# A recommender tower on one core: its dense layers in chunks of four units, sums turned to rows through memory

## What is computed

```python
e = jnp.stack([tbl_f[ids[:, f]] for f in range(16)], axis=1)      # 512 x 16 x 256
for i in range(3):
    z = jnp.einsum('bfe,bge->bfge', x, xk).reshape(B_, F_ * F_, E_)
    z = jnp.swapaxes(z, 1, 2)
    z = jnp.einsum('bcl,oc->bol', z, Ws[i]) + bs[i][None, :, None]
    z = jax.nn.relu(z)
    z = jnp.sum(z, axis=-1)
    outs.append(z)
    xk = jnp.broadcast_to(z[:, :, None], (B_, F_, E_))
h = jnp.concatenate([z, dense_ctx], axis=1)                       # 48 sums and 16 dense features
h = jnp.maximum(h @ W_top1 + b_top1, 0.0)                         # 64 -> 512
h = jnp.maximum(h @ W_top2 + b_top2, 0.0)                         # 512 -> 256
y = h @ W_top3                                                    # 256 -> 1
```

## Time and profile before

| | |
|---|---|
| median of 3 runs | 171.51 us (171.51 to 172.08) |
| the profiled execution | 171.46 us, span 169.6 us |
| PE busy | 137.1 us (81%) |
| DVE busy | 144.9 us (85%) |
| ACT busy | 126.3 us (74%) |
| POOL busy | 121.0 us (71%) |
| mean granted PE clock | 0.99 |

### The profile page before, as it was taken

One profiled execution on the slowest core, in us unless ns is written; L12 is line 12 of the kernel. 1 busy time (PEld: TensorE's weight loads), 2 busy tenths in 40 slices (PEclk: granted clock), 3 DMA queues, 4 the chain that ended last, 5 costly groups with the idle time before them and its releaser, 6 DMA issues.

```text
span 169.6 us, 6453 instructions
## 1 busy us (share of the span) xinstructions
PE 137.1 (81%) x2728; PEld 92.4 (54%) x2728; DVE 144.9 (85%) x136; ACT 126.3 (74%) x441; POOL 121.0 (71%) x84
## 2 busy tenths in 40 slices
PE   0045998988887878787879797999898999993995
PEld 0024665746464646464646464757474876763963
DVE  3169986999999999999999999999999998198330
ACT  3020465586979797979797979798999998977461
POOL 1777989898888888888888888989797995000000
PEclk9999999999999999999999999999999999999599
DMA  2343653131313030303030303031313100000000
GB/s 56 94 123 97 190 151 97 30 98 37 93 33 95 25 101 12 112 9 117 2 114 10 103 20 103 24 99 35 96 32 97 31 4 4 6 0 2 4 0 0
DMA packets 5273, 9.98 MB, mean 59 GB/s; under 512 B 2179, under 2 KB 2947, under 8 KB 5252
## 3 DMA queue, kind: packets, MB, share of 16 engines
q0 software_dynamic: 3072, 8.39, 17.2%
q1 hardware_dynamic: 2036, 1.29, 2.8%
q10 hardware_dynamic: 144, 0.00, 0.0%
HBM read 9.68 MB, written 0.00 MB: 57 GB/s over the span
## 4 chain that ended last, share of the span: by engine, by line
PE 46%; DVE 19%; ACT 18%; issue 8%; POOL 4%; DMA 3%; DVEq 1%; ACTq 0%
PE Y L627 25%; DVE PR L311 13%; ACT prod L387 8%; ACT XT L357 7%; PE T L592 5%; POOL X L329 4%; PE T L688 4%; PE ZB L648 4%; DVE prod L503 3%; PE Y L633 2%; ACT Y L378 2%; PE YD L670 2%; DMA X<-in_table,idx 2%; PE YD L688 2%; PE YD L604 1%
## 5 line engine op out<-in xcount | busy, mean ns | idle before, releaser
L311 DVE TENSOR_TENSOR PR<-T,XT 128x1024 f32<-128x1024 f32 (+2 forms) x72 | 101.1, 1450 | 7.0 <-ACT XT L357 6.9
L627 PE MATMUL Y<-PR,w_sb 128*32 128x272 f32 x1024 | 66.0, 399 | 13.0 <-DVE PR L311 12.6
L329 POOL DMA_INDIRECT X<-in_table,idx x64 | 61.2, 956 | 20.7 <-issue 16.1
L387 ACT ACTIVATE prod<-prod,bias_sb 128x256 f32<-128x256 f32 x122 | 60.1, 498 | 4.2 <-DVE prod L503 4.2
L311 POOL TENSOR_TENSOR PR<-XT 128x2048 f32<-128x2048 f32 (+2 forms) x16 | 59.7, 3734 | 0.3
L627 PEld LDWEIGHTS Y<-PR,w_sb 128*32 128x32 f32 x1024 | 31.1, 110 | 35.7 <-issue 12.1
L503 DVE TENSOR_TENSOR prod<-U,ZB 128x2048 f32<-128x2048 f32 (+1 forms) x18 | 35.6, 1982 | 3.4 <-PE ZB L648 3.3
L378 ACT ACTIVATE Y<-Y,bias 128x136 f32<-128x136 f32 x64 | 21.5, 336 | 14.2 <-PE Y L633 14.2
L592 PE MATMUL T<-ident_sb,X 128*128 128x128 f32 x128 | 21.7, 314 | 12.3 <-DMA X<-in_table,idx 12.3
L357 ACT ACTIVATE XT<-T 128x1024 f32<-128x1024 f32 (+1 forms) x17 | 16.6, 974 | 18.1 <-PE T L592 13.2
L592 PEld LDWEIGHTS T<-ident_sb,X 128*128 128x128 f32 x128 | 17.5, 211 | 14.0 <-issue 9.9
(11 more groups left out here) (48 smaller groups left out, 69.3 us busy)
## 6 DMA issues: line engine op xcount, KB each, us to landing
X<-in_table,idx POOLq DMA_INDIRECT x64, 2.8
w_sb<-in_w SPq DMA_DIRECT2D x1, 512.0 KB
w_sb<-in_w SPq DMA_DIRECT2D x1, 224.0 KB
sel_sb<-in_sel SPq DMA_DIRECT2D x1, 128.0 KB
ident_sb<-in_ident SPq DMA_DIRECT2D x1, 64.0 KB, 2.1
w1l_sb<-in_w1l SPq DMA_DIRECT2D x1, 64.0 KB
w2l_sb<-in_w2l SPq DMA_DIRECT2D x1, 64.0 KB
w_sb<-in_w SPq DMA_DIRECT2D x1, 64.0 KB
```

The source lines that it names most:

```text
L311: return eng.tensor_tensor(pr, x0.broadcast_to(shape), x1.broadcast_to(shape), ALU.mult)
L329: pool.indirect_dma_start(out=X[:, n % NV, g, :], out_offset=None, in_=table, in_offset=bass.IndirectOffsetOnAxis(ap=idx[:, NT * n + g:NT ...
L387: last = act.activation(q, q, ACT.Relu, bias=bias_sb[:, l + 1:l + 2], accum_out=to)
L627: pe.matmul(Y[TR * j:TR * j + TR, h, 0:YC], w0_sb[:, c, :], PR[:, v, h, c, CB * j:CB * (j + 1), :].rearrange("q b s -> q (b s)"), start=c ...
```

## The change

- The tower works on four chunks of four units. Chunks 0 and 1 run inside steps 7 to 10 and 11 to 14 (`part` 0 to 3), in a second PE loop; chunks 2 and 3 at the end. The second layer's four matmuls stand between the two contractions of a step, behind a wait for `u_read`.
- For chunks 0 and 1, and in part for 2 and 3, the sums reach `H` by two transfers, SBUF to memory and back as rows (`to_rows` on SP), in place of `select`. The bias of the first layer becomes a row of `w1`.
- The last chunk's second layer is contracted with the samples on the partitions, four matmuls of 256 columns, and DVE makes the third layer in one pass (`weighted`); the output leaves in two writes, the second of 128 rows of one number.
- POOL does no products for units 0 and 1, five rows for units 9 and 14, all eight for the last. After its last products it adds up two stages' products (`FOLDS`), which ACT summed before.
- `prod` has three buffers. PE has idle matmuls (`keep_busy`) at the start. Unit 2 is transposed before unit 1 is contracted. `layer_u` of the last unit is split, the last contractions follow each other, with spreads inside them.

```diff
-POOL_ROWS = {0: 0, NU - 2: 6, NU - 1: 6}
...
+POOL_FIRST = 2
+POOL_ROWS = {9: 5, 14: 5, NU - 1: 8}
...
+ACT_SHARE = {(NU - 2, 0): 2, (NU - 1, 1): 2, (NU, 1): 2, (NU - 3, 1): 0, (NU - 2, 1): 0}
+FOLDS = [(NU - 3, 1), (NU - 2, 1)]
...
+LOOP = range(3, FIRST)
+TOWER_LOOP = range(FIRST, NU - 1)
...
+            def to_rows(k, l, landed):
+
+                sp.dma_start(rows[k, l].rearrange("p (n b) -> p n b", b=SB), sums_of(k)[l])\
+                    .then_inc(sums_out[k], 16)
+                sp.wait_ge(sums_out[k], 16 * (l + 1))
+                sp.dma_start(H[TR * l:TR * l + F, PW * k:PW * (k + 1)].rearrange("q (g i) -> q g i", g=P // F),
+                             rows[k, l].rearrange("(g q) i -> q g i", q=F)).then_inc(landed, 16)
+
+            for k in range(NK):
+                sp.wait_ge(z0_ready, 2 * PC * (k + 1))
+                to_rows(k, 0, h_in if k < LAST else h_last_in)
+                if k < LAST:
+                    wait_sums(sp, (PC * (k + 1) - 1, 0))
+                    to_rows(k, 1, h_in)
+                if k < FLOW:
+                    wait_sums(sp, (PC * (k + 1), 1))
+                    to_rows(k, 2, h_in)
...
+            pool.wait_ge(bias_in, 16)
+            step = 0
+            for s, l in FOLDS:
+                b0 = act_share((s, l))
+                q = prod[:, s % NPR, SB * l + b0:SB * (l + 1), :, :].rearrange("q b f g -> q b (f g)")
+                if (s, l) == FOLDS[0]:
+                    pool.wait_ge(prod_ready, outer_done((s, l)))
+                    pool.tensor_scalar(q, q, bias_sb[:, l + 1:l + 2], 0.0, ALU.add, ALU.max)\
+                        .then_inc(pool_step, 1)
+                    step += 1
+                    pool.wait_ge(pool_step, step)
+                else:
+                    pool.wait_ge(relu_ready, FOLDS.index((s, l)))
+                pool.tensor_tensor(q[:, :, 0:P], q[:, :, 0:P], q[:, :, P:2 * P], ALU.add)\
+                    .then_inc(pool_step, 1)
+                step += 1
+                pool.wait_ge(pool_step, step)
+                pool.tensor_tensor(q[:, :, 0:P // 2], q[:, :, 0:P // 2], q[:, :, P // 2:P], ALU.add)\
+                    .then_inc(folded, 1)
...
+            sum_prod((NU - 4, 1), [0])
+            square(NU - 1)
+            read_behind(NU - 2)
+            read_u(NU - 2)
+            read_u(NU - 1, (0,))
+            sum_y(NU - 2, 0)
+            sum_prod((NU - 4, 1), [1])
+            sum_prod((NU - 3, 0), [0])
+            sum_y(NU - 2, 1)
+            sum_prod((NU - 3, 0), [1, 2, 3])
+            sum_prod((NU - 4, 1), [2])
             sum_y(NU - 1, 0)
-            sum_prod(NU - 2, 0)
+            sum_prod((NU - 2, 0))
+            sum_prod((NU - 4, 1), [3])
             sum_y(NU - 1, 1)
-            evacuate((1, HIDDEN1, 2))
-            evacuate((1, HIDDEN1, 3))
-            sum_prod(NU - 2, 1, [0, 1])
-            sum_prod(NU - 1, 0)
-            sum_prod(NU - 2, 1, [2, 3])
-            sum_prod(NU - 1, 1)
-            sum_prod(NU, 1)
-            evacuate((2, SELECT, 0))
-            evacuate((1, HIDDEN2, 0))
-            evacuate((1, HIDDEN2, 1))
-            evacuate((2, HIDDEN1, 0))
-            evacuate((2, HIDDEN1, 2))
-            evacuate((1, OUTPUT, 0))
-            evacuate((2, HIDDEN2, 0))
-            evacuate((2, OUTPUT, 0))
+            read_u(NU - 1, (1,))
+            relu_prod((NU - 2, 1))
+            read_selected(LAST - 1, 2)
+            sum_prod((NU - 1, 0))
+            read_hidden1(LAST - 1, 0)
+            read_hidden1(LAST - 1, 1)
+            sum_prod((NU - 1, 1))
+            sum_prod((NU, 1))
+            read_selected(LAST, 1)
+            read_selected(LAST, 2)
+            read_hidden2(LAST - 1, 0)
+            for c in range(2):
+                act.wait_ge(hidden1, 2 * LAST + 1)
+                act.activation(h1_of(LAST, c), hidden1_psum(LAST, 0)[:, c, :], ACT.Relu).then_inc(h1_ready, 1)
+            read_hidden2(LAST - 1, 1)
+            read_output(LAST - 1)
...
+            outer(NU - 2, [0], 0)
+            spread_z(NU - 2, 1)
+            spread_z(NU - 1, 0)
+            outer(NU - 2, [1], 1)
+            sum_prod((NU - 2, 0))
+            spread_z(NU - 1, 1)
+            outer(NU - 1, [0], 0)
+            outer(NU - 1, [0], 1)
+            outer(NU - 1, [1], 1)
+            sum_fold((NU - 3, 1))
             spread_z(NU)
-            outer(s, [1])
+            sum_prod((NU - 1, 1))
             outer(NU, [1])
-            sum_prod(NU, 1)
-            evacuate((2, HIDDEN1, 1))
-            evacuate((2, HIDDEN1, 3))
-            evacuate((2, HIDDEN2, 1))
+            sum_fold((NU - 2, 1))
+            sum_prod((NU, 1))
+            dve.wait_ge(weights_in, 16 * 7)
+            dve.wait_ge(hidden1, 2 * LAST + 2)
+            for c in range(2):
+                dve.tensor_scalar(h1_of(LAST, 2 + c), hidden1_psum(LAST, 1)[:, c, :], 0.0, None, ALU.max)\
+                    .then_inc(h1_dve, 1)
+            dve.wait_ge(hidden2, 2 * LAST + 1)
+            dve.scalar_tensor_tensor(out=weighted[:], in0=last_psum, scalar=0.0, in1=w3row_sb[:], op0=ALU.max,
+                                     op1=ALU.mult, accum_out=y_last[:]).then_inc(last_done, 1)
...
+            def step(n, v, r, k=None, part=None):
+
+                contract(n - 1, 1 - v, 0)
+                if isinstance(n, int) and n == 2:
+                    pe.wait_ge(spread_in, 16)
+                spread_rows(n - 2)
+                if part is not None and part >= 1:
+                    pe.wait_ge(u_read, n)
+                if part == 1:
+                    pe.wait_ge(h1_ready, 2 * k + 1)
+                    first_hidden(k, 1)
+                elif part in (2, 3):
+                    pe.wait_ge(h1_ready, 2 * k + 2)
+                    if part == 3:
+                        pe.wait_ge(h2_ready, 2 * k + 1)
+                    second_hidden(k, part - 2)
+                contract(n - 1, 1 - v, 1)
+                transpose(n + 1, 1 - v, r + v)
+                if part == 0:
+                    pe.wait_ge(weights_in, 16 * 7)
+                    pe.wait_ge(dense_in, 16)
+                    pe.wait_ge(h_in, 16 * 3 * (k + 1))
+                    pe.wait_ge(u_read, n)
+                    first_hidden(k, 0)
+                elif part == 1:
+                    pe.wait_ge(h1_ready, 2 * k + 2)
+                elif part == 2:
+                    pe.wait_ge(h2_ready, 2 * k + 1)
+                elif part == 3:
+                    pe.wait_ge(h2_ready, 2 * k + 2)
+                    outputs(k)
+                layer_u(n, v)
...
+            contract(0, 0, 0)
+            layer_u(0, 0)
+            contract(0, 0, 1)
+            transpose(2, 0, 1)
+            layer_u(1, 1)
+            pe.wait_ge(z0_ready, 2)
+            keep_busy(Y[:, 1, 0:P], 7)
...
+            layer_u(NU - 1, last, (0,))
+            contract(NU - 2, 1 - last, 0)
+            spread_rows(NU - 3)
+            contract(NU - 2, 1 - last, 1)
+            contract(NU - 1, last, 0, [(NU - 2, 0)])
+            contract(NU - 1, last, 1, [(NU - 2, 1), (NU - 1, 0)])
+            layer_u(NU - 1, last, (1,))
+            select(LAST - 1, 2)
+            spread_rows(NU - 1, 1)
+            pe.wait_ge(h_in, 16 * (3 * LAST - 1))
+            pe.wait_ge(h_ready, 1)
+            pe.wait_ge(y_done, LAST - 1)
             pe.wait_ge(u_read, NU)
-            for c in range(HC1):
-                tower((1, HIDDEN1, c))
-            spread_rows(NU - 1)
-            n0 = CHUNKS[2][0]
-            select(2, 0, n0, NU)
-            select(2, 1, n0, NU - 1)
-            select(2, 2, n0, NU - 2)
-            tower((1, HIDDEN2, 0))
+            for half in range(2):
+                first_hidden(LAST - 1, half)
             spread_rows(NU)
-            tower((1, HIDDEN2, 1))
-            select(2, 1, NU - 1, NU)
-            select(2, 2, NU - 2, NU).then_inc(mlp_psum[2], 1)
-            for c in range(HC1):
-                tower((2, HIDDEN1, c))
-            tower((1, OUTPUT, 0))
-            for c in range(HC2):
-                tower((2, HIDDEN2, c))
-            wait_sbuf(pe, (1, OUTPUT, 0))
-            tower((2, OUTPUT, 0))
+            pe.wait_ge(h1_ready, 2 * LAST)
+            second_hidden(LAST - 1, 0)
+            second_hidden(LAST - 1, 1)
+            pe.wait_ge(minus_half_ready, 2)
+            pe.matmul(last_psum, ones[:], b2row_sb[:], start=True, stop=False)
+            select(LAST, 1)
+            select(LAST, 2)
+            pe.wait_ge(h_last_in, 16)
+            pe.wait_ge(h_ready, 3)
+            for half in range(2):
+                first_hidden(LAST, half)
+            for q in range(HC1):
+                if q < 2:
+                    pe.wait_ge(h1_ready, 2 * LAST + 1 + q)
+                else:
+                    pe.wait_ge(h1_dve, q - 1)
+                tile = pe.matmul(last_psum, h1_of(LAST, q), w2_sb[:, q, :], start=False, stop=q == HC1 - 1)
+            tile.then_inc(hidden2, 1)
+            pe.wait_ge(h2_ready, 2 * LAST)
+            outputs(LAST - 1)
```

566 lines of the change are left out of this document (286 added, 280 removed).

## The result

The changed kernel takes **179.69 us** (median of 4 executions, 177.99 to 182.07); the kernel before took 171.80 on the same chip (4 executions, 171.51 to 172.10). The ratio is 1.039 with a 95% interval of 1.032 to 1.045: slower. I had said 169.7, 167.3 to 172.6, and 0.15 for slower. The ratios of this document leave out executions that were disturbed; the medians are over all. By mean granted clock the executions are 177.99 and 178.01 us at 0.967 and 0.968, and 181.37 and 182.07 at 0.948; a fifth, for the ratio alone, took 179.39 at 0.958.

A forecast was written before the change was run, and what follows sets the result against it. The prediction took VectorE (DVE) to bound the middle and a dependency chain the tail. From 171.46 us, terms -0.2, +4.0, +0.2, -2.4, -3.1 and +0.2 gave 170.2; half a microsecond off made 169.7, range 167.3 to 172.6.

The forecast's parts named there:

- The output: Final write: 128 rows of 4 bytes in place of one row take between 1.5 and 1.8 us, +0.2.
- The tower's waits: Steps 9, 10, 13, 14: late XT fills make DVE wait 1.3 and 1.1 us, in each of two rounds.
- such a fall in the tail: Tail: PE's clock falls to its lower level after thin work, slowing chunk 2's second-layer matmuls, +1.2 us.
- POOL's fifth row of unit 9: Unit 9's products: POOL takes five rows in place of four, saving DVE 0.57 us.
- The start: First units: more DVE product work, offset by a vanished idle before unit 2 and earlier transposes, -0.2 us.
- Contractions 14 and 15: Last two contractions, back to back with spreads inside: 10.0 us in place of 12.37, -2.4.
- The last chain: End of contractions to output's issue: 15.0 us in place of 18.1, a clock fall of 1.2 included, -3.1.
- rival A: Tail: the clock does not fall, so the kernel takes 168.5 us; chance 0.18.
- The memory pair: Sums written to memory and read back as rows: 4.2 us a pair, PE waits 0.6, +0.2 in all.
- Rival B: Steps 7 and 11: rows arrive late from memory, holding up PE; 171.2 or 173.2 us; chance 0.15.
- POOL's folds: Tail: folds of 2.0, 1.1 and 0.7 us end 2.5 us before DVE reduces, costing nothing.

The follow-up runs named there:

- e1: The changed kernel with its last 128 outputs turned into a row by one matmul and written in one write: 171.98 us, ratio to before 0.999.
- e4: The changed kernel writing its last 128 outputs 64 bytes apart into a scratch tensor: 211.2 us on a chip where the kernel before took 209.73.
- e8: The changed kernel writing its last 128 outputs as 64-byte rows, side by side, to a scratch tensor: 211.2 us where the kernel before took 209.73.
- e13: The changed kernel unedited, on a chip where the kernel before takes about 210 us: 219.44 us, ratio 1.042.
- e14: The changed kernel writing its last 128 outputs 64 bytes apart into a scratch tensor, same edit as e4, beside e13: 212.18 us, ratio 1.008.
- e3: The changed kernel with five idle matmuls ahead of the waits for U in steps 9, 10, 13 and 14: 176.52 us, ratio to before 1.023.
- e5: The changed kernel without the seven idle matmuls ahead of contract (1,0): 177.0 us, ratio to before 1.025.
- e17: The changed kernel with the output written as one row and chunks 0 and 1's second layer behind the transposes: 169.83 us, ratio to before 0.959.
- e18: The kernel of e17 without the seven idle matmuls ahead of contract (1,0): 165.28 us, ratio to before 0.963.

## Why the prediction was wrong

**The step that failed is *The output*.** I put 128 rows of 4 bytes between the output's 1.5 and the 1.8 of bias_sb and added 0.2; it cost 6.4. The bound came from the wrong side: bias_sb is 128 short rows read from memory and written to 128 partitions, this is a write into memory, whose pieces lie side by side. It took e1 to weigh it (6.3 us in the profile, 7.7 in the median with the clock's part), and e4, e8, e13 and e14 to rule out the number and the size of the pieces. This term alone put the time outside the range: with 0.2 true of the write the executions of 178.5 would have been 172.3, and e1 did take 171.98, both within 167.3 to 172.6. But that is no gain, and the long profiled execution would still have been 175.2; that the change is not faster has the reasons that follow.

**The tower's waits were right, but not the clock behind them.** Waits for the late fills: 4.8 predicted, 5.28 with the clock up. What I left out is that the same wait which delays the fill also leaves PE idle for a microsecond in a place where it has little else: I had forecast such a fall in the tail from the earlier trace rows and not asked for it at the waits that the change itself adds. It cost 3.3 us in the profiled execution (e3 against the changed kernel), 3.2 in the medians and 2.0 against the 178.5. Of the other 0.9 in e3's +5.1, 0.28 is unit 13's wait, and some 0.5 is POOL's fifth row of unit 9: the product is shorter (128x1536, 1.76), but zx still comes 8.49 behind the one before (80.78 to 89.27), 0.04 and not 0.57 sooner. The product itself starts only at 87.33, right behind its fill (86.20 to 87.23), and behind it DVE waits 0.19 for sums: there was hardly slack to win.

**The start.** -0.2 holds with the clock up (-0.1 in e3); the profiled execution lost 1.6 there to a fall behind the wait for a gather, which the seven idle matmuls made worse (e5). The kernel's 4 us between shortest and longest go with the mean clock, 0.967 against 0.948; which falls the other executions had, no trace shows.

**Contractions 14 and 15.** -1.8 for -2.4: they take 10.6 us in place of 10.0, and PE waits for nothing in them (busy 10.61 of 10.61 us). The two halves of unit 15, with spreads between their matmuls, take 2.3 and 2.5 by the profile's chain, not counting the spreads, where I had 2.16 each; the three spreads take the 1.1 that I had as 1.0 with waits.

**The last chain.** Both cases that I weighed happened. With the clock up it took 13.5 us (13.7 predicted, rival A), in e5 as well and with the row in e1 13.6; in e3, whose tail is the same code, the granted clock was 0.60 from 158 to 162 and it took 15.1 (15.0 predicted). So the working was right in either case, but the forecast counted on the fall, and the profiled execution had none: that its term is 1.5 better than -3.1 is luck. In e17 the fall was worse than either.

**The memory pair.** Rival B is false. The last pair of chunk 0 has its write issued at 73.03 and its read back at 74.46, 1.7 us to land, some 3.1 us in all (4.2 assumed), and the first layer stands behind the transposes at 76.32 with no wait. The same pair of chunk 1 (113.94, 115.36) made PE wait 0.46 at 117.12. The other pairs, whose writes have 512 pieces of 16 bytes, take 5.0 to 5.6 (the first 62.54, 66.33, and 1.7 to land), but PE never waits for those. The short pair of chunk 0:

```profile
73.03 0.34 SPq L311 DMA_DIRECT2D sums_rows<-z  x1
74.46 0.30 SPq L314 DMA_DIRECT2D H<-sums_rows  x1
```

**POOL's folds.** Nothing in time, as said, but not for the sizes given: 3.70 us in place of 2.0 for the first.

```profile
154.40 3.70 POOL L388 TENSOR_SCALAR prod<-prod,bias_sb 128x1024 f32<-128x1024 f32 x1
...
158.19 1.27 POOL L394 TENSOR_TENSOR prod<-prod 128x512 f32<-128x512 f32 x1
...
159.53 0.73 POOL L398 TENSOR_TENSOR prod<-prod 128x256 f32<-128x256 f32 x1
```

It ended at 160.26, and DVE reduces at 161.90, 1.6 later in place of 2.5.

**What the change is worth without its two faults** and the seven idle matmuls: 165.3 us (e18), 4% under the kernel before. The other parts together gain; no run takes the rows through memory, the chunks of four or the new tail out alone. Of the 13.2 us between e18 and the changed kernel's 178.5 the write of 4-byte pieces is 6.4 and the late fills some 5.3; the rest, by difference, is falls of the clock and the idle matmuls.

## What to carry to other kernels

Bound a transfer by rows of its own kind: direction, size of a piece and whether pieces touch in memory; at the very end of a kernel nothing covers it, and one matmul that turns a column into a row was 6.3 us cheaper than 128 adjacent 4-byte pieces. Where a change adds a wait to PE, price the clock behind the wait too, and expect its fall in some executions only. In this kernel a matmul that nobody waits for belongs behind the transposes, not ahead of them, as the next unit's fill is the path.

## What the chip showed that I had not expected

- 128 pieces of 4 bytes: 7.9 us from issue to the span's end when adjacent in the output, 1.8 when 64 bytes apart in a scratch tensor (e4: 207.57 to 209.4), 1.8 with 64 bytes each (e8: 207.51 to 209.3). The 512 pieces of 16 bytes of `sums_rows<-zz` took 3.6 to land.
- Two chips took 210 us for the kernel that the others run in 172. Instructions last as long there (a product of 2048 elements 2.29 us), but PE stops inside runs of matmuls, with nothing to wait for that the profile shows: 24 times among the U matmuls of e13, 17.6 us in all. PE's timeline of e13:

```profile
86.41 0.72 PE L717 MATMUL YD<-XT,w1l_sb 128*32 128x64 f32 x18
88.26 0.32 PE L717 MATMUL YD<-XT,w1l_sb 128*32 128x64 f32 x5 [1.13 <-issue]
89.73 0.33 PE L717 MATMUL YD<-XT,w1l_sb 128*32 128x64 f32 x7 [1.15 <-issue]
```

  On the other chips the same 32 records take 0.65 us in one piece. What stops PE there stays open.
- A TENSOR_SCALAR of 1024 elements on POOL took 3.70 us, as long as its TENSOR_TENSOR of 2048.
